# A two-layer kernel whose first six tiles are loaded as whole rows and turned by TensorE, with input order 8p+m in the first layer

## The reference, cut to what matters

```python
# x: (8, 256, 1024) float32; E = 8, R = 16, TOP_K = 2
# layer 0
base   = einsum('btd,od->bto', x, W)                   # W: (1024, 1024)
logits = einsum('btd,ed->bte', x, Wr) + 5.0 * one_hot(language_ids)[:, None, :]
gates  = softmax over the two largest logits, 0 for the other six
h      = einsum('btd,erd->bter', x, A)                 # A: (8, 16, 1024)
lora   = einsum('bter,bte,eor->bto', h, gates, B)      # B: (8, 1024, 16)
x = x + base + 2.0 * lora
# layer 1
w = weight[adapter_ids]                                # (8, 1024, 1024)
x = x + einsum('bsi,boi->bso', x, w)
```

## Time and profile before

| | us |
|---|---|
| median of 3 runs | 405.83 |
| lowest and highest run | 404.25, 407.34 |
| the profiled execution: its own time | 405.14 |
| the profiled execution: its span | 403.3 |

### The profile page before, as it was taken

One profiled execution on the slowest core, in us unless ns is written; L12 is line 12 of the kernel. 1 busy time (PEld: TensorE's weight loads), 2 busy tenths in 40 slices (PEclk: granted clock), 3 DMA queues, 4 the chain that ended last, 5 costly groups with the idle time before them and its releaser, 6 DMA issues.

```text
span 403.3 us, 5968 instructions
## 1 busy us (share of the span) xinstructions
PE 395.0 (98%) x1920; PEld 333.3 (83%) x1920; DVE 315.1 (78%) x408; ACT 171.0 (42%) x231; POOL 57.8 (14%) x84
## 2 busy tenths in 40 slices
PE   8999989999999999999999999999999999999996
PEld 8989868888889988888888888888888888878884
DVE  2899999998348477329777967999989898999910
ACT  1452333664220142335355334556555555565621
POOL 1010101300000100000210112323113130225200
PEclk9999999999999999999999999999999999999999
DMA  8977420133276400006686999999999999999231
GB/s 187 230 210 205 138 80 0 53 106 105 81 232 199 115 0 2 1 0 188 134 291 224 288 260 303 276 303 279 294 300 304 274 257 284 265 259 271 65 104 52
DMA packets 78577, 72.79 MB, mean 180 GB/s; under 512 B 7090, under 2 KB 77266, under 8 KB 77522
## 3 DMA queue, kind: packets, MB, share of 16 engines
q1 hardware_dynamic: 51584, 47.21, 47.2%
q10 hardware_dynamic: 26962, 25.21, 19.7%
HBM read 55.61 MB, written 16.78 MB: 179 GB/s over the span
## 4 chain that ended last, share of the span: by engine, by line
PE 85%; DVE 7%; issue 2%; DMA 2%; SPq 2%; POOL 0%; ACT 0%; DVEq 0%
PE banks L1166 14%; PE banks L1168 14%; PE banks L1167 14%; PE banks L1069 11%; PE banks L1070 11%; PE banks L1071 11%; PE banks L1062 4%; DVE weights L480 2%; PE banks L1081 2%; PE banks L1082 2%; DVE turned_w_f L468 2%; PE banks L1080 2%; SPq L380 2%; DMA raw<-in_x_dram 1%; DMA raw<-in_L_cond_W_dram 1%
## 5 line engine op out<-in xcount | busy, mean ns | idle before, releaser
L1069 PE MATMUL banks<-ring,weights 128*128 128x512 f32 x192 | 75.1, 391 | 1.7 <-DVE weights L480 1.7
L1166 PE MATMUL banks<-weights,tokens 128*128 128x512 f32 x176 | 68.7, 390 | 1.0 <-issue 1.0
L427 POOL TENSOR_TENSOR raw<-raw,ident 128x128 f32<-128x128 f32 x50 | 35.1, 702 | 237.7 <-DMA raw<-in_L_cond_weight_dram 199.1
L936 ACT ACTIVATE weights<-weights_f 128x1024 fp32r<-128x1024 f32 x44 | 46.5, 1060 | 52.4 <-DVE weights_f L618 49.8
L1168 PE MATMUL banks<-weights,tokens 128*128 128x512 f32 x176 | 68.5, 389 | 0.0
L1167 PE MATMUL banks<-weights,tokens 128*128 128x512 f32 x176 | 68.5, 389 | 0.0
L618 DVE STREAM_TRANSPOSE weights_f<-raw 128x1024 f32<-128x1024 f32 x42 | 51.8, 1235 | 9.9 <-POOL raw L427 9.4
L624 DVE TENSOR_TENSOR weights<-weights_f,weights 128x1024 fp32r<-128x1024 f32 x44 | 52.8, 1202 | 1.7 <-ACT weights L936 1.6
L1070 PE MATMUL banks<-tokens,weights 128*128 128x512 f32 x128 | 49.8, 389 | 0.0
L1071 PE MATMUL banks<-ring,turned_w 128*128 128x512 f32 x128 | 49.8, 389 | 0.0
L1069 PEld LDWEIGHTS banks<-ring,weights 128*128 128x128 f32 x192 | 36.1, 188 | 9.6 <-DVE weights L480 2.1
(11 more groups left out here) (115 smaller groups left out, 625.7 us busy)
## 6 DMA issues: line engine op xcount, KB each, us to landing
raw<-in_L_cond_weight_dram SPq DMA_DIRECT2D x168, 128.0 KB, 5.6
ring_f<-in_L_cond_weight_dram SPq DMA_DIRECT2D x88, 128.0 KB, 5.9
raw<-in_x_dram SPq DMA_DIRECT2D x64, 128.0 KB, 3.3
x_kept<-stage ACTq DMA_DIRECT2D x32, 256.0 KB, 4.1
out_dram<-sums ACTq DMA_DIRECT2D x32, 256.0 KB, 6.6
raw<-in_L_cond_W_dram SPq DMA_DIRECT2D x32, 128.0 KB, 3.0
sums<-x_kept ACTq DMA_DIRECT2D x3, 1024.0 KB, 8.9
stage<-x_kept ACTq DMA_DIRECT2D x3, 1024.0 KB, 9.7
```

Of the source, the lines that this page charges most:

```text
L427: nc.gpsimd.tensor_tensor(spot, spot, ident[:].rearrange("p (q j) -> p q j", q=Q), ALU.add)\
L936: nc.scalar.activation(w1_dest(n, 0), w1_turn(n).rearrange("p (m f) -> p m f", m=M), ACT.Copy)\
L1069: nc.tensor.matmul(ps, u_hi, x_hi, start=first and k == 0, stop=False, skip_group_check=True)
L1166: nc.tensor.matmul(l1_bank(o), x_hi, w_hi, start=m == 0, stop=False)
```

## The change

The first six tiles (A, x tiles 0 to 3, W tile 0: `FRONT`) are loaded by one transfer each, 128 partitions by a whole row of 4 KB, into six places of their own (the three raw slots and three pieces of the ring), with nothing to wait for. TensorE turns each with eight transposes of 128x128 into two PSUM banks (`turn_front`); a transpose takes every eighth column, so that input d = 8p+m lands at partition p, block m. ScalarE copies A, x tiles 1 and 3 and W tile 0 out of PSUM, VectorE x tiles 0 and 2 (`copy_front`). All other tiles of the first layer are loaded as before, and VectorE's turn of them reads every eighth element (`"p (q j m) -> p q m j"`), which gives the same input order. `features(0, 0)` is taken apart and set between the transposes. `WARM` goes from 44 to 12, `FILL` goes. `make_t1` of span 0 moves from VectorE to GpSimd. ScalarE copies product 1 out of PSUM for all four r ahead of the four high parts of `("x", 0, 6, t)`.

```diff
@@ -29,8 +29,7 @@
-    WARM = 44
-    FILL = 12
+    WARM = 12
@@ -66,8 +65,12 @@
-    LOADS = ([("a",)] + [x_item(0, 0, t) for t in range(XT)] + [("w", m) for m in range(HM)] +
-     [x_item(0, 1, t) for t in range(XT)] + [("w", m) for m in range(HM, M)] + [("b",)] +
+    FRONT = [("a",)] + [x_item(0, 0, t) for t in range(XT)] + [("w", 0)]
+    FRONT_AT = {item: k for k, item in enumerate(FRONT)}
+    FRONT_BANK = (0, 2, 6, 0, 2, 6)
+    LOADS = ([("w", m) for m in range(1, HM)] + [x_item(0, 1, t) for t in range(XT)] + [("w", m) for m in range(HM, M)] + [("b",)] +
      [x_item(1, h, t) for h in range(2) for t in range(XT)])
@@ -80,7 +83,7 @@
-    BEFORE[item] = here[k - 1] if k else None
+    BEFORE[item] = here[k - 1] if k else FRONT[s] if s < RAW else None
@@ -215,8 +218,14 @@
+def front_ps(item):
+    at = FRONT_BANK[FRONT_AT[item]]
+    return banks[:, at:at + 2, :]
+def front_tiles(item):
+    return front_ps(item).rearrange("p b (m f) -> p (b m) f", f=P)
@@ -273,6 +282,10 @@
+front_loaded = [sem(f"front_loaded{k}") for k in range(len(FRONT))]
+front_turned = sem("front_turned")
+front_copied_act = sem("front_copied_act")
+front_copied_dve = sem("front_copied_dve")
@@ -380,15 +393,25 @@
+    def load_front(k):
+        item = FRONT[k]
+        if item[0] == "a":
+            rows = a_rows[:, :]
+        elif item[0] == "x":
+            rows = x_rows[item[3] * P:(item[3] + 1) * P, :]
+        else:
+            rows = w0.rearrange("(q m s) d -> m q s d", m=M, s=S)[0]
+        sp.dma_start(raw_tile(k), rows).then_inc(front_loaded[k], 16)
     def load(item):
-        if BEFORE[item]:
+        if BEFORE[item] in FRONT_AT:
+            sp.wait_ge(front_turned, FRONT_AT[BEFORE[item]] + 1)
+        elif BEFORE[item]:
             sp.wait_ge(transposed, TURN_AT[BEFORE[item]] + 1)
...
                              b_pairs[c]).then_inc(raw_loaded[SLOT[item]], 16)
-        elif item[0] == "a":
-            fill(item, a_rows[:, :].rearrange("(q s) d -> s q d", s=S))
         elif item[0] == "x":
@@ -403,6 +426,8 @@
+    for k in range(len(FRONT)):
+        load_front(k)
     for item in LOADS:
@@ -427,9 +452,29 @@
-    for m in range(HM):
+    def make_t1(t):
+        pool.wait_ge(transposed, TURN_AT[x_item(0, 1, t)] + 1)
+        pool.wait_ge(featured, featured_at(0, 0, t) + 1)
+        if t == 0:
+            pool.wait_ge(lo_done, PIECE_AT["wt", HM - 1] + 1)
+        else:
+            pool.wait_ge(t2_done, t)
+        nc.gpsimd.tensor_tensor(half_x(0, t, 0), half_x(1, t, 0), half_x(0, t, 0), ALU.subtract)\
+            .then_inc(t1_done, 1)
+    pool.wait_ge(front_loaded[FRONT_AT["w", 0]], 16)
+    spot = raw_tile(FRONT_AT["w", 0]).rearrange("p (q m j) -> p m q j", q=Q, m=M)[:, 0]
+    nc.gpsimd.tensor_tensor(spot, spot, ident[:].rearrange("p (q j) -> p q j", q=Q), ALU.add)\
+        .then_inc(ones_added, 1)
+    for m in range(1, HM):
         add_ones(("w", m))
-    for r in range(HM):
+    make_t1(0)
+    make_t1(1)
+    make_t1(2)
+    add_ones(("w", HM))
+    make_t1(3)
+    for r in range(1, HM):
         add_ones(("w", HM + r))
@@ -457,16 +502,12 @@
             return
-        if item[0] == "a":
-            nc.vector.transpose(fac[:, :, 0:ER].rearrange("p m (q s) -> p q m s", q=Q),
-                                src.rearrange("p (q m j) -> p q m j", q=Q, m=M)).then_inc(transposed, 1)
-            return
         if item[0] == "x":
...
         nc.vector.transpose(dst.rearrange("p (m q s) -> p q m s", m=M, q=Q),
-                            src.rearrange("p (q m j) -> p q m j", q=Q, m=M)).then_inc(transposed, 1)
+                            src.rearrange("p (q j m) -> p q m j", q=Q, m=M)).then_inc(transposed, 1)
@@ -528,6 +569,8 @@
         dve.wait_ge(lo_done, PIECE_AT["wt", r] + 1)
+        if r == 0:
+            dve.wait_ge(front_copied_act, 4)
         a11, a21 = quarter_w(7, r), quarter_w(5, r)
@@ -624,47 +667,44 @@
-    turn(("a",))
-    turn(x_item(0, 0, 0))
+    def copy_front(t):
+        dve.wait_ge(front_turned, FRONT_AT[x_item(0, 0, t)] + 1)
+        nc.vector.tensor_copy(tokens_f[:, t].rearrange("p (b f) -> p b f", b=2), front_ps(x_item(0, 0, t)))\
+            .then_inc(front_copied_dve, 1)
     dve.wait_ge(wr_loaded, Q * 16)
-    nc.vector.transpose(fac[:, :, ER:ER + S], wr_raw.rearrange("p (m j) -> p m j", m=M)).then_inc(fac_done, 1)
-    turn(x_item(0, 0, 1))
-    low(("xt", 0))
+    nc.vector.transpose(fac[:, :, ER:ER + S], wr_raw.rearrange("p (j m) -> p m j", m=M)).then_inc(fac_done, 1)
     dve.wait_ge(consts, 3)
...
     nc.vector.tensor_copy(lang_f[:], lang_i[:]).then_inc(setup, 1)
-    turn(x_item(0, 0, 2))
     dve.wait_ge(setup, 2)
...
                             lang_f[:].unsqueeze(2).to_broadcast([P, NB, E]), ALU.is_equal).then_inc(setup, 1)
-    low(("xt", 1))
     dve.wait_ge(setup, 3)
     nc.vector.tensor_scalar(bias[:], bias[:], LANG_BIAS, None, ALU.mult).then_inc(setup, 1)
-    turn(x_item(0, 0, 3))
+    copy_front(0)
+    low(("xt", 0))
+    copy_front(2)
+    low(("xt", 1))
     low(("xt", 2))
-    turn(("w", 0))
     low(("xt", 3))
+    low(("wt", 0))
     turn(("w", 1))
-    low(("wt", 0))
     turn(("w", 2))
...
     low(("wt", 3))
-    make_t1(0, 0)
     turn(x_item(0, 1, 1))
     make_t2(0, 0)
-    make_t1(0, 1)
     turn(x_item(0, 1, 2))
...
     make_t2(0, 1)
-    make_t1(0, 2)
     turn(x_item(0, 1, 3))
...
     make_t2(0, 2)
-    make_t1(0, 3)
     turn(("w", 4))
@@ -796,8 +836,12 @@
-        if kind == "xt":
-            act.wait_ge(transposed, TURN_AT[x_item(0, 0, p[1])] + 1)
+        if kind == "xt" and p[1] % 2 == 0:
+            act.wait_ge(front_copied_dve, p[1] // 2 + 1)
+        elif kind == "xt":
+            act.wait_ge(front_copied_act, p[1] // 2 + 2)
+        elif kind == "wt" and p[1] == 0:
+            act.wait_ge(front_copied_act, 4)
         elif kind == "wt":
@@ -952,21 +996,32 @@
-    for t in range(XT):
-        high(("xt", t))
+    def copy_front(item):
+        act.wait_ge(front_turned, FRONT_AT[item] + 1)
+        if item[0] == "a":
+            dst, src = fac[:, :, 0:ER], front_tiles(item)
+        else:
+            dst = (tokens_f[:, item[3]] if item[0] == "x" else turned_wf[:, 0])
+            dst, src = dst.rearrange("p (b f) -> p b f", b=2), front_ps(item)
+        nc.scalar.activation(dst, src, ACT.Copy).then_inc(front_copied_act, 1)
+    copy_front(("a",))
+    high(("xt", 0))
+    copy_front(x_item(0, 0, 1))
+    high(("xt", 1))
+    copy_front(x_item(0, 0, 3))
+    high(("xt", 2))
+    high(("xt", 3))
+    copy_front(("w", 0))
     high(("wt", 0))
...
     high(("wt", 3))
-    copy_p1(0, 0)
-    copy_p1(0, 1)
-    high(("x", 0, 6, 0))
-    high(("x", 0, 6, 1))
-    copy_p1(0, 2)
-    high(("x", 0, 6, 2))
-    copy_p1(0, 3)
-    high(("x", 0, 6, 3))
+    for r in range(HM):
+        copy_p1(0, r)
+    for t in range(XT):
+        high(("x", 0, 6, t))
     copy_h(0, 1)
@@ -1049,18 +1104,42 @@
-    def features(s, h):
+    def turn_front(item):
+        k = FRONT_AT[item]
+        if item[0] == "w":
+            pe.wait_ge(ones_added, 1)
+            pe.wait_ge(front_copied_act, 2)
+        else:
+            pe.wait_ge(front_loaded[k], 16)
+        if item == x_item(0, 0, 2):
+            pe.wait_ge(front_copied_act, 1)
+        elif item == x_item(0, 0, 3):
+            pe.wait_ge(front_copied_dve, 1)
+        rows = raw_tile(k).rearrange("p (k m) -> p m k", m=M)
+        for m in range(M):
+            turn = nc.tensor.transpose(front_tiles(item)[:, m], rows[:, m], ident[:])
+        turn.then_inc(front_turned, 1)
+    def feature(s, h, t):
         if s == 0 and h == 0:
-            pe.wait_ge(fac_done, 1)
-        for t in range(XT):
+            if t == 0:
+                pe.wait_ge(fac_done, 1)
+            if t % 2 == 0:
+                pe.wait_ge(front_copied_dve, t // 2 + 1)
+            pe.wait_ge(front_copied_act, (1, 2, 2, 3)[t])
+        else:
             if s and t % 2 == 0:
...
             pe.wait_ge(transposed, TURN_AT[x_item(s, h, t)] + 1)
-            xT = tokens_f[:, h * XT + t].rearrange("p (m f) -> p m f", m=M)
-            ps = banks[:, feature_bank(s, h, t), (t % 2) * FC:(t % 2 + 1) * FC]
-            for m in range(M):
-                mm = nc.tensor.matmul(ps, xT[:, m, :], fac[:, m, 0:FC], start=m == 0, stop=m == M - 1)
-            mm.then_inc(featured, 1)
+        xT = tokens_f[:, h * XT + t].rearrange("p (m f) -> p m f", m=M)
+        ps = banks[:, feature_bank(s, h, t), (t % 2) * FC:(t % 2 + 1) * FC]
+        for m in range(M):
+            mm = nc.tensor.matmul(ps, xT[:, m, :], fac[:, m, 0:FC], start=m == 0, stop=m == M - 1)
+        mm.then_inc(featured, 1)
+    def features(s, h):
+        for t in range(XT):
+            feature(s, h, t)
@@ -1100,6 +1179,7 @@
                 step(0, 1, k, r, main_bank(0, r), True)
+        pe.wait_ge(front_copied_act, 4)
         features(0, 1)
@@ -1135,9 +1215,16 @@
-    features(0, 0)
-    for _ in range(FILL):
```

(11 more changed lines are left out.)

## The result

The changed kernel takes **421.77 us** (median of 6 runs, 417.1 to 422.54) against 405.63 for the kernel before on the same chip: ratio 1.0357, 95% interval 1.0308 to 1.0406. It is 3.6% slower, 11 us above the top of my range. The profiled execution took 421.81 with a span of 420.0; its mean granted clock is 0.984, where before had 1.0.

What follows compares the result with a forecast made beforehand. The start of TensorE's product 6, decided by VectorE's chain, was taken as the bound: 51.7 in place of 54.73, 3.0 us earlier, so 405.14 becomes 402.1, and 402.8 as median. Range for 8 in 10: 401.0 to 410.5.

Steps and rivals of the forecast that it cites:

- the price of the stepped turn: VectorE's eleven turns before product 6, reading every eighth float: taken as no extra cost, upper bound 0.77 us each.
- the turn of B: VectorE turn writing with a 512-byte step, 2.004 us: gave the upper bound, 0.77 more than a turn of x.
- the rival of the dear turns: Each VectorE turn takes 0.77 us more, product 6 at 57.4, time 408.5 to 410; chance 0.33.
- 8-element row: VectorE instruction reading with the same step, 168 ns for 8 elements: the ground for pricing the step at nothing.
- the eight stepped turns of span 1: VectorE's turns in span 1: claimed to cost nothing, since VectorE idles there between TensorE's releases.
- The landing of W tile 0: Transfers in the front: 4 KB runs at some 350 GB/s, 1.5 us per tile, W tile 0 landed at 12.1.
- rival of slow transfers: Runs of 4 KB no faster than 1 KB: W tile 0 at 16.4, product 1 at 22.2, 406.1 us; chance 0.07.
- TensorE's front without a gap: TensorE from 8.8 us: four features and three turns make 10.0 us, product 1 at 18.9 in place of 23.59.
- front slower: TensorE's clock falls or stepped weight loads cost half their bound: product 1 and product 6 2 us later, 404.8; chance 0.15.
- (1): ScalarE's four product 1 copies precede product 6's first high part, so VectorE waits 1.9 us before its low part.
- (2): GpSimd's make_t1 takes 1.29 us in VectorE's chain before product 6: period 2.65 against 3.01, winning 0.36 per tile.

Runs made afterwards that it cites:

- e7: e3 with ScalarE's instructions in the order of the kernel before (inputs mixed, timing only): 405.26 us, ratio 0.9993.
- e10: e7 with VectorE's first copy and low part ahead of the language bias and 4 identity matmuls ahead of the first features (timing only): 402.08 us, ratio 0.9893.
- e11: e10 with VectorE's turns reading every eighth float again, so that it computes the reference: 412.91 us, ratio 1.0167.
- e4: The kernel before, with only VectorE's first-layer turns (A, Wr, x, W) reading every eighth element: 420.76 us, ratio 1.0361.
- e2: The changed kernel with VectorE's turns reading contiguous runs, no step (inputs mixed, timing only): 414.17 us, ratio 1.0206.
- e3: The changed kernel with both W tile 0 in four transfers and VectorE's turns without step (inputs mixed, timing only): 409.34 us, ratio 1.0092.
- e1: The changed kernel with W tile 0 loaded by four transfers of 32 rows in place of one: 413.66 us, ratio 1.0201.
- e6: The kernel before, with only ScalarE's four copies of product 1 put ahead of the four high parts for product 6: 409.63 us, ratio 1.0099.
- e5: The kernel before, with only the four subtractions t1 moved from VectorE to GpSimd: 403.82 us, ratio 0.9975.
- e8: e3 with 40 identity matmuls between TensorE's front steps and VectorE's first copy ahead of the language bias (timing only): 416.45 us, ratio 1.027.

## Why the prediction was wrong

**The failed step is the price of the stepped turn.** I took nothing, from the row of an 8-element instruction, and kept 0.77 from the turn of B as the upper bound. It is 0.87. Eleven such turns stand ahead of product 6. What that costs is read from product 1 to product 6, in the profiled executions (that of e7 is the longest of its ten); "new order" is ScalarE's order of the change:

| run | product 1 | product 6 | between | time |
|---|---|---|---|---|
| before | 23.59 | 54.73 | 31.1 | 405.1 |
| e7, no step | 23.46 | 54.72 | 31.3 | 407.6 |
| e10, no step, tight front | 20.68 | 51.98 | 31.3 | 402.1 |
| e11, step | 20.93 | 60.28 | 39.4 | 413.1 |
| e4, step | 26.15 | 65.56 | 39.4 | 420.1 |
| e2, no step, new order | 29.37 | 61.98 | 32.6 | 414.3 |
| e3, no step, new order | 23.54 | 56.84 | 33.3 | 409.2 |
| e1, step, new order | 21.72 | 61.23 | 39.5 | 412.5 |
| the change, step, new order | 29.39 | 66.64 | 37.3 | 421.8 |

The forecast had 32.8 between the two (51.7 - 18.9), which e2 and e3, without the step, bear out. With ScalarE's old order the step adds 8.1 us (e10 to e11). With the new order it adds 6.2 (e3 to e1), for the slow turns cover the wait for ScalarE, 1.41 in e3 and 0.38 in e1. In the changed kernel VectorE waits for neither ScalarE nor GpSimd behind its first low part of W.

So the rival of the dear turns had the mechanism: it added 5.7 (57.4 - 51.7), and its 38.5 between the two products is 1.0 short of e1, about eleven times the 0.1 by which its price was low. That its time, at most 410, is still too low for the changed kernel has other reasons: product 1 came 10.5 us later than it assumed, the slow passes cost about 2.4 in place of its 1.5, and the second layer had 1.9 us more of issue waits. Even e11, with the front mended, has product 1 2.0 us later than it assumed, and 412.9. That the eight stepped turns of span 1 cost nothing is borne out: of the 2.7 us that e11 loses against e10 behind product 6, the slow passes make 2.5.

The 8-element row misled in a way that could have been seen: 168 ns for 8 elements is the fixed part of an instruction, in which a penalty per element of about 0.85 ns (0.87 us over 1024) is 7 ns. A difference of two short rows cannot carry a product of eleven long ones. Of my two bounds, the one from an instruction of the same kind and length was 0.1 off.

**The landing of W tile 0 was a second failed step**, one that no rival had. I multiplied one rate by the bytes and did not look at the shape of the access pattern. In the changed kernel it cost about as much as the step: 8.1 us by e1 (421.8 to 413.7), with the cold features behind the wait as part. Of the 9.3 us between the two profiled executions 5.4 stand ahead of product 6; behind it, e1 has none of the 2.9 us of issue waits, and why is not shown. My rival of slow transfers had the place, at 22.2, but as a matter of run length, which was not the cause: the five transfers ahead of it ran at 323 GB/s.

**TensorE's front without a gap was optimistic.** I had 10.0 us from 8.8 to product 1 at 18.9. In e10, with every fault mended, product 1 starts at 20.68: the copy of x0 waits until 8.63, the first feature starts at 10.22, and warm-up takes over a us longer than forecast, since it does not reach the pace of the earlier trace rows: in the changed kernel the window from 5 to 7 us has 12 instructions, where before had 20, at a clock of 1.00 in both. In the changed kernel and e3 VectorE's language bias stood ahead of that copy and waited for a small transfer until 9.94. Before, that wait cost nothing; the change made VectorE's first copy urgent and left the bias in front of it. The rival "front slower" with the clock fall was borne out in e3 and e7; e7 to e10 says 3.2 us.

**The two waits that I had worked out.** (1), ScalarE's order, forecast at 1.9 us: 1.63, 1.41 and 1.54 in e2, e3 and e6, and none in the changed kernel, where the slow turns cover it. Right in mechanism, too cheap in consequence: e3 to e7 is 4.1 us, and e6 against before 4.0 to 4.7. The clock that falls behind the longer wait at product 6 is part of it (about 1.4 us in e3, whose passes start 0.43 apart up to 59.96), issue waits in the second layer are another. (2), GpSimd's t1: 1.29 as forecast; where the orders are good it wins about 1 us (e5). In e10 VectorE's turns beside it took 1.23 to 1.25, as elsewhere, and the one low part that began beside it 0.91 in place of 0.68.

**The method held where its inputs did.** With step, landing and bias mended (e10), product 6 starts at 51.98 against my 51.7 and the kernel takes 402.08 against my 402.8. That is partly luck: two errors (product 1 1.8 late, and no wait for ScalarE, its order being the old one) about cancel. And e10 mixes the orders of the inputs: TensorE's transposes read one constant step, and with loads in 1 KB runs per 32 partitions only a step of 8 floats gives VectorE the same order. So the step is what the change, as it is written, has to pay, and e11, the best form of it run here that computes the reference, loses 1.7%. One way out stands untested: transposes of the first six tiles that read four runs of 32 floats, 256 apart, would give the input order of the kernel before, and VectorE's turns would need no step. No run here shows whether TensorE takes such an operand, or at what price.

How much of 16 us belongs to which cause depends on what else is mended. In us, by medians and by the ratios to the kernel before times 405 (the two runs of a row are not always from one chip):

| mended | from, to | medians | ratios |
|---|---|---|---|
| landing | the change, e1 | 8.1 | 6.3 |
| step | the change, e2 | 7.6 | 6.1 |
| step | e1, e3 | 4.3 | 4.4 |
| step | e11, e10 | 10.8 | 11.1 |
| step | e4, before | 15.8 | 14.6 |
| ScalarE's order | e3, e7 | 4.1 | 4.0 |
| bias behind the copy, 4 identities | e7, e10 | 3.2 | 4.1 |

What causes the second layer's issue waits stays open. They are 1.0 us before, none in e1, 0.4 to 3.0 elsewhere, and do not follow the front: e4 and e6, with the front of the kernel before, have 2.5 and 2.7.

## What to carry to other kernels

When a layout change puts a step into an operand of the busiest vector engine, price it by an instruction of the same kind and length, never by a short one; multiply by the count up to the join, and let nothing hide but a wait that the sum has on the same engine (here 1.4 us). Before counting bytes over bandwidth, read the outermost dimension of every new transfer. An engine with a wait of some us ahead of it can pay twice, for the wait and for a slow restart, so a new delay just before a join that already waits can cost more than its own length; and when work is moved off an engine, what was harmless at the head of its queue must be looked at again.

## What the runs showed of the hardware

- VectorE's 128x1024 fp32 turn, by the distance of the floats read: 1.23 us at 4 and 8 bytes, 2.01 at 16, 2.11 at 32.
- One 512 KB transfer whose source had an outermost dimension of 4 took 17.7 us behind five others, with a DMA share of 0.35 in its last 3 us; split by that dimension it had landed about seven us sooner, and the three tiles behind it five to six us sooner.
- TensorE's transposes read the same 32-byte step and show no price for it: their weight loads took 188 to 191 ns, those of the contiguous identity in the kernel before 190 to 192, though the contiguous ones of the earlier trace rows took 140; 24 transposes took 2.84 to 3.01 us, 24 contiguous identity matmuls 2.84 (e8).
- TensorE's granted clock behind a rest does not follow its length alone. It stayed 1.00 behind rests of 0.99 (e10), 1.66 (before), 1.83 (the change) and 2.15 us (e11). It fell behind 1.79 in e4 (0.57 from 27 to 31 us, 12 instructions where e11 has 18) and 2.20 in e1; behind 2.73 and 2.57 us (e3, e7) the stretch from 10 to 15 us shows 0.72 and 0.66; behind 4.50 and 6.29 us the changed kernel's rows show 0.50, which is 1.2 GHz. What else decides between 1.8 and 2.2 us is open.
